# Setup and layer 0 of a cross-attention stack as one unrolled stream of pairs, with GpSimd scaling probabilities, and context halves made in layer 1

## The reference

```python
def layer0(x_c, x_s, Wn, bn, Wm, bm, Wl, bl, Wo, bo):      # x_c = x, x_s = ctx; C = 64, T = 256
    inorm = lambda x: (x - mean(x)) * rsqrt(var(x) + 1e-5)  # over the last axis
    conv  = lambda W, b, x: einsum('oc,bct->bot', W, x) + b[None, :, None]
    Mn, Mm = conv(Wn, bn, inorm(x_c)), conv(Wm, bm, inorm(x_s))
    A  = softmax(einsum('bct,bcs->bts', Mn, Mm), axis=-1)   # [32, 256, 256]
    Mo = einsum('bcs,bts->bct', conv(Wl, bl, x_s), A)
    return conv(Wo, bo, Mo) + x_c
# layer 1: two 16-head cross attentions (head width 128) of x on ctx, with a bias key and value, then an MLP with gelu
# layer 2: grouped attention (32 heads on 8) and layer norm;  layer 3: latent attention, RMS norm and an MLP
```

## Time and profile before

| | us |
|---|---|
| median of 3 runs | 1674.97 (1672.3 to 1674.98) |
| profiled execution, its own time | 1674.09 |
| its span in the trace | 1672.4 |
| PE busy | 1545.5 (92% of the span) |
| DVE busy | 1103.6 (66%) |
| ACT busy | 672.5 (40%) |
| POOL busy | 454.6 (27%) |

### The profile page before, as it was taken

How to read it: one execution, slowest core, us unless ns; L and a number is a source line. 1 busy time by engine, 2 the same in 40 slices (tenths; PEclk the granted TensorE clock), 3 DMA queues, 4 the chain that set the end, 5 groups by cost and what they waited for, 6 DMA issues and landing times. The chain is left out here.

```text
span 1672.4 us, 33255 instructions
## 1 busy us (share of the span) xinstructions
PE 1545.5 (92%) x13291; PEld 1321.8 (79%) x13291; DVE 1103.6 (66%) x2377; ACT 672.5 (40%) x1270; POOL 454.6 (27%) x533
## 2 busy tenths in 40 slices
PE   4988999999999999999999999799788869999797
PEld 2656888888888888888888888789667748887697
DVE  6886666666666776667666666555499945776443
ACT  4654433343433434333333334332366634454221
POOL 2004020020110221200201110232288866562110
PEclk9998999999999999999999999999899979999899
DMA  4000010010000000000100000000410000000001
GB/s 131 1 0 26 14 39 14 1 39 14 27 13 14 26 14 14 26 14 13 39 14 9 31 26 11 20 20 0 84 56 1 2 1 2 3 2 2 1 1 50
DMA packets 44466, 34.12 MB, mean 20 GB/s; under 512 B 10658, under 2 KB 41384, under 8 KB 44200
## 3 DMA queue, kind: packets, MB, share of 16 engines
q1 hardware_dynamic: 44328, 32.17, 6.7%
HBM read 30.00 MB, written 2.10 MB: 19 GB/s over the span
## 5 line engine op out<-in xcount | busy, mean ns | idle before, releaser
L964 DVE STREAM_TRANSPOSE att_pt<-att_prob 32x256 f32<-32x256 f32 x496 | 215.7, 435 | 6.4
L864 ACT ACTIVATE split_q_sb<-psum,g_cols 128x512 f32<-128x512 f32 x128 | 88.3, 690 | 321.7 <-PE psum L732 321.7
L781 PE MATMUL psum<-att_wo_hi,att_ot_hi 128*128 128x256 f32 x512 | 149.2, 291 | 2.5 <-DVE att_ot_lo L977 1.4
L935 DVE TENSOR_REDUCE att_rmax<-psum 128x6 f32<-128x390 f32 (+1 forms) x96 | 49.2, 513 | 151.3 <-PE psum L694 151.3
L781 PE MATMUL psum<-att_wo_lo,att_ot_hi 128*128 128x256 f32 x512 | 144.6, 282 | 0.0
L781 PE MATMUL psum<-att_wo_hi,att_ot_lo 128*128 128x256 f32 x512 | 144.6, 282 | 0.0
L764 PE MATMUL psum<-att_pt,att_v_sb 128*128 128x128 f32 x1024 | 128.6, 279 | 3.5 <-DVE att_ot_lo L977 3.5
L987 DVE TENSOR_TENSOR g_x_res<-psum,g_x_res 128x256 f32<-128x256 f32 x128 | 54.3, 424 | 114.7 <-PE psum L781 88.3
L764 PEld LDWEIGHTS psum<-att_pt,att_v_sb 128*128 128x128 f32 x1024 | 122.9, 193 | 7.9 <-DVE att_ot_lo L977 3.7
L867 ACT ACTIVATE att_k_sb<-psum,g_cols 128x512 f32<-128x512 f32 x128 | 88.1, 688 | 80.9 <-PE psum L732 80.9
L732 PE MATMUL psum<-split_feat_hi,split_wide_hi 128*128 128x512 f32 x256 | 103.7, 405 | 4.5 <-DVE split_feat_lo L1011 3.3
(11 more groups left out here) (287 smaller groups left out, 3944.8 us busy)
## 6 DMA issues: line engine op xcount, KB each, us to landing
g_ctx_f<-in_L_xattn_wq SPq DMA_DIRECT2D x32, 128.0 KB, 2.2
g_ctx_f<-in_L_xattn_wk SPq DMA_DIRECT2D x32, 128.0 KB, 2.3
g_ctx_f<-in_L_xattn_wv SPq DMA_DIRECT2D x8, 512.0 KB, 3.8
g_ctx_f<-in_L_xattn_wo SPq DMA_DIRECT2D x8, 512.0 KB, 3.8
c_ctx_tok<-in_ctx SPq DMA_DIRECT2D x4, 512.0 KB, 5.6
g_x_res<-in_x SPq DMA_DIRECT2D x4, 512.0 KB, 8.7
g_w<-in_L_xattn_mlp_w SPq DMA_DIRECT2D x2, 1024.0 KB
out<-g_x_res SPq DMA_DIRECT2D x1, 2048.0 KB, 7.5
```

Of the source, the lines that this page charges most:

```text
L781: mm = pe.matmul(o_ps[p % 2], a, b, start=(h == 0 and t == 0), stop=(not last and h == HG - 1 and t == 2))
L864: act.activation(q_sb[:, h, :], q_ps[:, :], ACT.Identity, bias=G.cols[:, layer, head:head + 1]).then_inc(q_ready, 1)
L935: dve.tensor_reduce(rmax[:, a:b], s_ps[group][:, :, :], X_AXIS, ALU.max).then_inc(max_done, 1)
L964: turned = dve.transpose(pt[to:to + 32, :, :, r, u, 32 * a:32 * a + 32].rearrange("p h a t -> p (h a) t"), by_pair[of:of + 32, :, u, 32 * ...
```

## The change

- `phase_setup` is gone. `phase_layer0` loads ctx and x in six chunks of 1, 1, 2, 4, 4 and 4 pairs; the small weights are issued after the first two chunks.
- Statistics are taken pair by pair, three pairs ahead (`statistics(u + 3)` in step u); GpSimd makes `rstd` for two pairs at a time (`invert_deviation`), and normalises x pair by pair (`normalize`), ScalarE ctx.
- GpSimd scales the four probability tiles (`scale`), VectorE no longer does; GpSimd's copy of ctx is gone, TensorE reads ctx itself. The loop is unrolled.
- The transposes and halves of ctx move into layer 1: one block of 512 tokens in each of the steps j = -1, 0, 1, 2 (`turn_context`, two ScalarE copies, `low_context`); ctx is loaded a second time for it, 512 KB a block, the last three by SyncE in layer 1. The projections, scores and `bias_outputs` of these steps wait for `ctx_ready`.

The core of the diff (left out: names and buffers, the constants' transpose, which comes after pair 6, and the lines that only move):

```diff
+                def tokens(q):
+                    a, b = CHUNKS[q]
+                    sp.dma_start(ctx_tok[:, a:b, :], c_dram[:, a:b, :]).then_inc(ctx_in[q], 16)
+                    sp.dma_start(G.x_res[:, a:b, :], x_dram[:, a:b, :]).then_inc(x_in[q], 16)
+                tokens(0)
+                tokens(1)
                 sp.wait_ge(w_zero, 1)
...
+                for q in range(2, len(CHUNKS)):
+                    tokens(q)
...
+                def invert_deviation(k):
+                    pool.wait_ge(mv_done, 4 * (k + 1))
+                    if k >= 2:
+                        pool.wait_ge(cn_done, 2 * (k - 1))
+                    r, var = (t.rearrange("p u s -> p (u s)") for t in (rstd[:, k % 2, :, :], mv[:, k % 2, :, :, 1]))
+                    pool.tensor_scalar(r, var, 1e-5, None, ALU.add).then_inc(eps_added, 1)
+                    pool.wait_ge(eps_added, k + 1)
+                    pool.tensor_tensor(r, r, G.minus_half[:, 0:4], ALU.pow).then_inc(rstd_done, 1)
+
+                def normalize(u):
+                    k = u // 2
+                    pool.wait_ge(rstd_done, k + 1)
+                    if u >= 4:
+                        pool.wait_ge(mix_psum, u - 3)
+                    pool.tensor_scalar(xn[:, u % 4, 0, :], G.x_res[:, u, :], mv[:, k % 2, u % 2, 0, 0:1], rstd[:, k % 2, u % 2, 0:1],
+                                       ALU.subtract, ALU.mult).then_inc(xn_done, 1)
+
+                def scale(u):
+                    pool.wait_ge(rsum_done, u + 1)
+                    for i in range(4):
+                        sc = pool.tensor_tensor(prob[u % 2][:, i // 2, i % 2, :], prob[u % 2][:, i // 2, i % 2, :],
+                                                rsum[:, u % 2, i:i + 1].to_broadcast([P, D]), ALU.mult)
+                    sc.then_inc(prob_done, 1)
+
...
+                invert_deviation(0)
+                normalize(0)
+                for u in range(PAIRS):
+                    if u % 2 == 0 and u + 2 < PAIRS:
+                        invert_deviation(u // 2 + 1)
+                    if u + 1 < PAIRS:
+                        normalize(u + 1)
+                    scale(u)
...
+                for u in range(PAIRS + 2):
+                    front, r = u < PAIRS, u - 2
+                    if front:
+                        pe.wait_ge(xn_done, u + 1)
+                        pe.wait_ge(cn_done, u + 1)
+                        if u:
+                            pe.wait_ge(mix_done, u)
+                        for i in range(2):
+                            mm = pe.matmul(mix_ps[:, i, :], w_t[:, i, :], xn[:, u % 4, i, :], start=True, stop=True)
+                        mm.then_inc(mix_psum, 1)
+                    if r >= 0:
+                        pe.wait_ge(prob_done, r + 1)
+                        if r:
+                            pe.wait_ge(t_act, r)
+                            pe.wait_ge(t_dve, r)
+                        for b in range(2):
...
+                def normalize(u):
+                    k = u // 2
+                    act.wait_ge(shift_done, k + 1)
+                    if u >= 4:
+                        act.wait_ge(mix_psum, u - 3)
+                    act.activation(xn[:, u % 4, 1, :], ctx_tok[:, u, :], ACT.Identity, bias=shift[:, k % 2, u % 2:u % 2 + 1],
+                                   scale=rstd[:, k % 2, u % 2, 1:2]).then_inc(cn_done, 1)
...
+                def statistics(u):
+                    k = u // 2
+                    if k >= 2 and u % 2 == 0:
+                        dve.wait_ge(xn_done, 2 * (k - 1))
+                    for i, (src, arrive) in enumerate(((G.x_res, x_in), (ctx_tok, ctx_in))):
+                        dve.wait_ge(arrive[chunk(u)], 16)
+                        dve.bn_stats(stats[:, u % 4, i, :], src[:, u, :]).then_inc(stats_done, 1)
+                    for i in range(2):
+                        dve.wait_ge(stats_done, 2 * u + i + 1)
+                        dve.bn_aggr(mv[:, k % 2, u % 2, i, :], stats[:, u % 4, i, :]).then_inc(mv_done, 1)
+
+                def shifts(k):
+                    dve.wait_ge(rstd_done, k + 1)
+                    if k >= 2:
+                        dve.wait_ge(cn_done, 2 * (k - 1))
+                    dve.scalar_tensor_tensor(shift[:, k % 2, :], mv[:, k % 2, :, 1, 0], -1.0, rstd[:, k % 2, :, 1],
+                                             ALU.mult, ALU.mult).then_inc(shift_done, 1)
...
+                statistics(0)
+                statistics(1)
+                shifts(0)
...
+                for u in range(PAIRS + 2):
+                    front, r = u < PAIRS, u - 2
+                    if u % 2 and u + 1 < PAIRS:
+                        shifts(u // 2 + 1)
+                    if r >= 0:
+                        dve.wait_ge(t_psum, 2 * r + 2)
+                        dve.tensor_copy(prob_t[:, 1, :, :], t_ps[1][:, :, :]).then_inc(t_dve, 1)
+                    if front:
+                        if u:
+                            dve.wait_ge(exp_done, 4 * u)
+                        for b in range(2):
+                            dve.wait_ge(s_psum, 2 * u + b + 1)
+                            dve.tensor_reduce(nmax[:, b, :], s_ps[b][:, :, :], X_AXIS, ALU.max, negate=True).then_inc(max_done, 1)
+                    if u + 3 < PAIRS:
+                        statistics(u + 3)
+                    if r >= 0:
+                        dve.wait_ge(o_psum, r + 1)
+                        if r == 0:
+                            dve.wait_ge(w_ready, 1)
+                        dve.scalar_tensor_tensor(G.x_res[:, r, :], o_ps[:, :], obias[:, 0:1], G.x_res[:, r, :],
+                                                 ALU.add, ALU.add).then_inc(x_done, 1)
+                        dve.wait_ge(x_done, r + 1)
+                        dve.bn_stats(G.stats[:, r, :], G.x_res[:, r, :])
+                    if front:
+                        dve.wait_ge(exp_done, 4 * u + 4)
+                        if u >= 2:
+                            dve.wait_ge(prob_done, u - 1)
+                        dve.reciprocal(rsum[:, u % 2, :], ssum[:, u % 2, :]).then_inc(rsum_done, 1)
+                        dve.wait_ge(y_psum, u + 1)
+                        dve.tensor_copy(y_sb[u % 2][:, :, :], y_ps[:, :, :]).then_inc(y_done, 1)
...
-                            for i in range(4):
-                                sc = dve.tensor_scalar(prob[q][:, i // 2, i % 2, :], prob[q][:, i // 2, i % 2, :],
-                                                       rsum[:, i:i + 1], None, ALU.mult)
-                            sc.then_inc(prob_done, 1)
...
+                    for b in range(1, NBLK if g == 0 else 0):
+                        sp.wait_ge(ctx_psum, KT * b)
+                        sp.dma_start(w.ctx_blk[:, :, :], w.ctx_dram[:, PPB * b:PPB * (b + 1), :]).then_inc(ctx_in, 16)
...
+                    if j < NBLK - 1:
+                        pe.wait_ge(ctx_ready, KT * (j + 2))
...
+                    if j < NBLK and h == 0:
+                        pe.wait_ge(ctx_ready, KT * (j + 1))
...
+                def turn_context(b, j):
+                    if b:
+                        pe.wait_ge(ctx_in, 16 * b)
+                        pe.wait_ge(ctx_ready, KT * b)
+                    if j > 0:
+                        pe.wait_ge(shifted, len(GROUPS) * j)
+                    if j > 1:
+                        pe.wait_ge(ot_ready, PPB * (j - 1))
+                    for k in range(KT):
+                        for i in range(PPB):
+                            mm = pe.transpose(x_ps[k][:, i * P:(i + 1) * P], w.ctx_blk[:, i, k * P:(k + 1) * P], G.ident[:, :])
+                        mm.then_inc(ctx_psum, 1)
...
+                    if g == 0:
+                        pe.wait_ge(ctx_ready, KT * NBLK - KT)
...
+                        if h == 0 and -1 <= j < NBLK - 1:
+                            turn_context(j + 1, j)
...
+                        if h == 0 and -1 <= j < NBLK - 1:
+                            for k in range(KT):
+                                act.wait_ge(ctx_psum, KT * (j + 1) + k + 1)
+                                act.activation(G.ctx_hi[:, k, (j + 1) * BLK:(j + 2) * BLK], x_ps[k], ACT.Copy).then_inc(ctx_high, 1)
...
+                def low_context(b):
+                    cols = slice(b * BLK, (b + 1) * BLK)
+                    for k in range(KT):
+                        dve.wait_ge(ctx_high, KT * b + k + 1)
+                        dve.tensor_tensor(G.ctx_lo[:, k, cols], x_ps[k], G.ctx_hi[:, k, cols].bitcast(F32), ALU.subtract).then_inc(ctx_ready, 1)
...
+                    if -1 <= j < NBLK - 1:
+                        low_context(j + 1)```

GpSimd's list in layer 0. Before, one step of the loop for two pairs; `l_c_fix` is the copy of ctx:

```order
L306 ISA [waits l0_y_psum]
L306 COPY l_c_fix<-c_ctx_tok 128x256
L306 ISA [waits l0_y_psum]
L306 COPY l_c_fix<-c_ctx_tok 128x256
L308 REGISTER_ALU
```

(3 more changed lines are left out.)

356 lines of the change are left out of this document (114 added, 242 removed).

## The result

The changed kernel took 1699.88 us (median of 4 runs, 1695.96 to 1701.25), the kernel before beside it 1674.61 (4 runs): ratio 1.0150, 95% interval 1.0137 to 1.0163. It is slower by 25.3 us. The profiled execution took 1695.96, its span is 1694.3, both 21.9 above those of before.

The account below looks back on a forecast made before the run. TensorE and VectorE were taken to share layer 0's limit, TensorE to bound from layer 1 on. Layer 0 +4.5, then 7.3 + 2.7 + 1.0, gave +15.5 on 1674.09: 1690 us; own range 1684 to 1697, 8-in-10 range 1681 to 1702.

Parts of the forecast that it names:

- VectorE held up: Rival, layer 0: GpSimd's scalings hold up VectorE twice per two pairs, +8 us, 1698; chance 8%.
- the clock low nearly throughout: Rival, layer 0: busy stretches don't bring TensorE's clock back, two pairs grow by 3 to 5 us, 1705 and more; 10%.
- Term 1: Start of layer 0: first projection of pair 0 at 17.5 us instead of 34.40, -16.9 us.
- Term 2: Layer 0, even to odd pair: x queues behind GpSimd's deviations; 7.6 us, so two pairs take 12.1 instead of 9.8.
- The first double step: Layer 0's first two-pair step: -1 us for the missing back half, +3.5 for TensorE's low clock at the start.
- Term 3: Layer 0, TensorE's clock: +9 us, 3.5 at the start and 1.0 in each of six two-pair steps; bounds 0 and about double.
- Term 4: Layer 1's first projection waits for VectorE's low halves of ctx block 0, behind weight split and memsets: +6.9, 0.4 of clock.
- Term 5: Layer 1: ctx transposes in TensorE's stream, 0.9 us for each of three blocks, +2.7.
- Term 6: Layer 1, step j = 1: wait before `bias_outputs` for block 2's low halves, made behind `turn`, +1.0 us.
- The clock holds: Rival, layer 0: TensorE stays at 2.4 GHz once there, the clock costs only 3.5 us, total 1684; 12%.
- GpSimd's wait is hidden: Rival, layer 0: odd pairs' projections never wait for GpSimd, a pair keeps 4.88 us, layer 0 ends at 107.5, total 1668; 8%.

Follow-up runs that it names:

- e1: Changed kernel with GpSimd normalising the next pair's x ahead of the deviations instead of behind them; 1669.86 us, ratio 0.9982 to the kernel before.
- e3: Changed kernel with five unneeded TensorE products in each odd step, ahead of the wait for normalised x; 1691.31 us.
- e2: Changed kernel with GpSimd's normalisation of x only subtracting the mean, without the product with the deviation (does not compute the layer); 1695.56 us.
- e4: Changed kernel with VectorE's low halves of ctx block 0 ahead of the value weights' split and the memsets; 1697.93 us.
- e10: Changed kernel with ScalarE normalising x, ctx block 0's low halves and block 1's load earlier, and later low halves before `turn`; 1660.30 us.
- e7: Changed kernel with ctx block 0's low halves ahead of the weights' split and SyncE's load of block 1 ahead of its wait; 1695.98 us.
- e11: Changed kernel with ScalarE normalising x, block 0's low halves and block 1's load earlier, extra TensorE transposes in setup and layer 1's start; 1659.05 us.
- e5: Changed kernel with ScalarE instead of GpSimd normalising x, and VectorE's shift covering x and ctx; 1665.48 us, ratio 0.9958.
- e6: Changed kernel with ScalarE normalising x and VectorE doing the four scalings, GpSimd keeping only the deviations; 1669.12 us, ratio 0.9978.

## Why the prediction was right, and where its sizes were off

The direction, the mechanism and the range (1681 to 1702) held; the point, 1690, was 10 us low, all of it in layer 0, which was to cost +4.5 and cost +15.4. That the stated range held is in part luck. The forecast's own range, 1684 to 1697, was missed by 3 us; the top was set at 1702 for two rivals, VectorE held up and the clock low nearly throughout, and neither came true.

- **Term 1**, first projection at 17.5: 17.07. Right, and with it the gain of 17 us.
- **Term 2**, the crux: the wait of the odd pair's x behind the deviations, behind the next statistics, behind this pair's scores. Rows show each link (scores 2.04 after the projection, aggregates, L198, L207), and e1 shows that the order is the cause: 30.4 us of layer 0, more than its whole loss, hang on two swapped calls. The scaling was priced well (0.6, measured 0.61). **The normalisation was mis-sized**: 0.45 taken, bounds 0.40 to 0.73, measured 1.23, outside both. The rest of the chain came out 0.2 shorter (maxima and statistics took 2.17 us, 81.14 to 83.31, for 2.34), so the even-to-odd step was 8.17 instead of 7.6. At full clock a double step is 12.86 (e3) instead of 12.1. I had taken the one-input copy as the neighbour of an instruction that reads two numbers per partition, and no row of such a form on GpSimd with a wide tile stood in the trace; by e2 even one number makes it 0.93.
- **The first double step**, "-1" for the missing back half plus 3.5 for the start: 16.03 instead of 14.6. All of it but the wait of 3.78 ran at half clock.
- **Term 3**, the clock: right in kind (six low stretches for six double steps), 1.0 us per double step taken, 1.97 on average by e3, 0.1 of it not the clock's. The bound "about double" was the value.
- Together: 0.4 less for the start, 1.4 more in the first double step, 6 x (0.76 + 0.97) = 10.4 more in the others, 0.4 less in the drain (17.8 for 18.2): 11.0, as 15.4 less 4.5.
- **Term 4**, 17.8 us from layer 0's end: 17.7, released by VectorE's low halves. The price was right; the 0.4 of clock did not come, since the clock rose 3.5 us after the first projection and 3.6 before the change. The tacit reading that this wait was the only one was not: e4 shows SyncE's load right behind it. "Nothing hides it" held; it hid something else.
- **Term 5**, 0.9 each: 0.8. **Term 6**, 1.0: 0.76 to 0.8 (e10 removes it).
- **Rivals.** *The clock holds* is refuted by the rows of 0.50. *GpSimd's wait is hidden* would have given 1668; e1, where no odd pair waits for it (even ones still do, for 4.3 us in all), gave 1669.9, with a double step of 10.47, just below the 10.6 from which that rival was to decide. Its condition was not met in the changed kernel; its sum held to 2 us (layer 0's end 109.5 for 107.5), because a shorter start and drain made good part of the longer steps, 10.47 for 9.76. *VectorE is held up by GpSimd*: its long instructions kept their lengths (maxima 685 and 686 ns, addition to `x_res` 484 and 456 before and after). *Low clock nearly throughout*: 0.85 granted from 34.7 to 127.2; not so.
- In term 2 the bound for dearer scalings, 8.2 of 12.1, adds up to 8.1; nothing hangs on it.

The Trainium skill, "TensorE: Matmul & The Clock Gate", section on oscillation, said that matmul groups cut by waits fall back to the low clock again and again. The trace and e3 agree, with six falls, at 1.97 us each on average.

## What to carry to other kernels

An engine taken for nearly free is free only in load: ask of each instruction that is put on it what stands ahead of it in its list, and what that waits for. Here one swap in the order of a helper engine's list was worth 28 us by the ratios and 30 at the mark, more than any price. Where a wait goes, look at once for what was hidden behind it (a load behind another wait in SyncE's list, with the low clock after it: e4 kept 1.2 of 5.6 us, e7, without that wait, 4.6 of 5.7), and count an idle TensorE twice, for the wait and for the low clock after it.

## What the runs showed of the hardware

- GpSimd on 128x256 float32: product with a broadcast column 0.61 us, subtraction of one number per partition as TENSOR_SCALAR 0.93, subtraction and product with two numbers 1.23. The form with fewer full operands is the dearer one.
- In the changed kernel TensorE's granted clock fell to half in or soon after each idle stretch of 3.17 to 3.33 us, and in the experiments it also fell soon after shorter ones: 1.96 us in e3 (u = 7), 2.00 in e4, 2.18 and then 0.71 in e11. It did not fall after 1.63 us in e1 or after 1.16 in e3. Once fallen, it stayed low for 3.4 or 6.8 us in layer 0, though TensorE was busy 3.40 of 3.40 and 5.81 of 6.80 us of two such stretches.
- VectorE beside GpSimd: the copy to high halves of the value weights took 1.75 us while GpSimd split weights, and 0.68 in e4, where it came after them (first two rows below, changed kernel and e4). The Trainium skill, "SBUF — State Buffer", section "Who interferes with whom", says that VectorE's fast copies are blocked by GpSimd; the two rows agree. The tiny `shift`, which reads two SBUF tiles, took 0.57 us in e5 beside a scaling (six of the seven in the steady part; third row), 0.15 in e6, where GpSimd does not scale, but 0.15 to 0.16 in the changed kernel beside GpSimd's normalisation (fourth row). So it was held by the one form and not by the other.

```profile
150.58 1.75 DVE L1051 CAST att_wv_hi<-g_ctx_f 128x1024 fp32r<-128x1024 f32 x1
```
```profile
151.70 0.68 DVE L1052 CAST att_wv_hi<-g_ctx_f 128x1024 fp32r<-128x1024 f32 x1
```
```profile
65.20 0.57 DVE L334 SCALAR_TENSOR_TENSOR l_shift<-l_mv,l_rstd 128x4 f32<-128x4 f32 x1 [0.26 <-POOL l_rstd L200]
```
```profile
84.79 0.16 DVE L344 SCALAR_TENSOR_TENSOR l_shift<-l_mv,l_rstd 128x2 f32<-128x2 f32 x1 [0.27 <-POOL l_rstd L200]
```
